# Filling rep straight from dt and u in SBUF, and the second product by x behind the routing of rows

## The reference, cut to what matters

```python
xn   = layernorm(x)
xc   = silu(conv4(xn @ W_in[:1024].T));  gate = silu(xn @ W_in[1024:].T)
ts, Bm, Cm = split(xc @ W_x.T)               # each normalised by its rms
dt   = softplus(ts @ W_dt.T + b_dt)
# for each step: state = state * exp(dt * A) + (dt * xc) * B ;  y = sum over 16 states of state * C
s    = ((y + xc * D) * gate) @ W_out.T
out  = x + s * silu(mixture_of_experts(xn))
```

## Time and profile before

| | us |
|---|---|
| median of 3 runs (1052.16 to 1054.01) | 1053.31 |
| the profiled execution | 1050.33 |
| its span, first to last instruction | 1048.4 |
| DVE busy in the span | 983.2 |
| POOL busy | 904.9 |
| PE busy | 853.0 |
| ACT busy | 728.4 |

### The profile page before, as it was taken

How to read it: one execution, slowest core, us unless ns; L and a number is a source line. 1 busy time by engine, 2 the same in 40 slices (tenths; PEclk the granted TensorE clock), 3 DMA queues, 4 the chain that set the end, 5 groups by cost and what they waited for, 6 DMA issues and landing times.

```text
span 1048.4 us, 10364 instructions
## 1 busy us (share of the span) xinstructions
PE 853.0 (81%) x2756; PEld 317.2 (30%) x2756; DVE 983.2 (94%) x1027; ACT 728.4 (69%) x1281; POOL 904.9 (86%) x320
## 2 busy tenths in 40 slices
PE   8945458989878998999746859989888979988478
PEld 5321113333323343333211313333323323323123
DVE  6779999999999999999999899999999997999996
ACT  3656757888877767888664566888778775767543
POOL 0616899989989998998898988899988989999996
PEclk9986669999989999999976869999999998999778
DMA  9948559887779666675843753866548575664735
GB/s 335 350 154 311 203 200 354 294 298 272 264 271 336 226 226 243 240 276 203 282 116 144 212 209 121 309 236 233 203 178 308 204 255 191 237 237 171 283 54 144
DMA packets 86585, 245.93 MB, mean 235 GB/s; under 512 B 9344, under 2 KB 10752, under 8 KB 79872
## 3 DMA queue, kind: packets, MB, share of 16 engines
q1 hardware_dynamic: 67712, 197.03, 53.0%
q10 hardware_dynamic: 12672, 31.46, 7.6%
q0 software_dynamic: 6144, 16.78, 6.0%
HBM read 183.11 MB, written 62.13 MB: 234 GB/s over the span
## 4 chain that ended last, share of the span: by engine, by line
POOL 22%; DVE 21%; PE 20%; issue 12%; ACT 12%; DMA 10%; SPq 2%; ACTq 0%; DVEq 0%; POOLq 0%
POOL drive L605 13%; DVE sc_ps L1207 7%; DMA rep<-rep_rows 5%; POOL drive L618 4%; ACT sc_ps L818 4%; DVE drive L1207 4%; DVE drive L1217 4%; PE x_ps L1532 3%; PE dt_ps L1460 3%; DMA rep_rows<-dtu 3%; PE f_ps L1485 3%; PE y_ps L1500 2%; PE x_ps L1396 2%; POOL slot_x L569 2%; POOL moe L590 1%
## 5 line engine op out<-in xcount | busy, mean ns | idle before, releaser
L605 POOL TENSOR_TENSOR drive<-rep,b_all 128x2048 f32<-128x2048 f32 x127 | 579.6, 4603 | 37.6 <-DMA rep<-rep_rows 34.0
L818 ACT ACTIVATE sc_ps<-rep,a_neg 128x512 f32<-128x512 f32 x512 | 332.2, 681 | 101.8 <-DVE drive L1217 72.1
L1500 PE MATMUL y_ps<-drive,stack 128*32 128x512 f32 x1024 | 151.6, 668 | 104.1 <-DVE drive L1217 66.2
L618 POOL TENSOR_TENSOR drive<-drive,c_all 128x1024 f32<-128x1024 f32 x92 | 219.8, 2389 | 11.8 <-ACT state L797 9.7
L1207 DVE TENSOR_TENSOR_SCAN sc_ps<-sc_ps,state,drive 128x512 f32<-128x512 f32 x164 | 202.5, 1272 | 5.6 <-ACT sc_ps L818 3.9
L1207 DVE TENSOR_TENSOR_SCAN sc_ps<-sc_ps,drive 128x512 f32<-128x512 f32 x164 | 193.5, 1214 | 10.2 <-ACT sc_ps L818 6.1
L1217 DVE TENSOR_TENSOR drive<-sc_ps,c_all 128x1024 f32<-128x1024 f32 x164 | 199.2, 1215 | 2.8
L1485 PE MATMUL f_ps<-w_ring,xT_slot 128*128 128x512 f32 x368 | 173.0, 614 | 23.4 <-ACT xT_slot L828 22.9
L1460 PE MATMUL dt_ps<-xnT,w_g 128*128 128x512 f32 x232 | 125.1, 689 | 24.1 <-ACT dtu L785 24.1
L1207 DVE TENSOR_TENSOR_SCAN drive<-sc_ps,state,drive 128x512 f32<-128x512 f32 x92 | 113.7, 1267 | 6.6 <-ACT sc_ps L818 6.6
L1207 DVE TENSOR_TENSOR_SCAN drive<-sc_ps,drive 128x512 f32<-128x512 f32 x92 | 109.7, 1208 | 2.0 <-POOL drive L605 0.9
(11 more groups left out here) (189 smaller groups left out, 1048.8 us busy)
## 6 DMA issues: line engine op xcount, KB each, us to landing
rep<-rep_rows SPq DMA_DIRECT2D x128, 512.0 KB, 6.2
w_ring<-wring SPq DMA_DIRECT2D x46, 1024.0 KB, 6.3
rep_rows<-dtu ACTq DMA_DIRECT2D x32, 512.0 KB, 3.1
x_slot<-slot_x SPq DMA_DIRECT2D x46, 256.0 KB, 6.7
slot_rows<-y_slot ACTq DMA_DIRECT2D x46, 256.0 KB, 4.4
w_g<-wg_in SPq DMA_DIRECT2D x32, 256.0 KB, 7.1
w_x<-wx_in SPq DMA_DIRECT2D x24, 256.0 KB, 4.3
slot_x<-zeros SPq DMA_DIRECT2D x1, 5888.0 KB, 20.6
```

The lines of the kernel that those rows point to most:

```text
L605: pool.tensor_tensor(drive[:, m % RING, :, :], rep[:, n % 2, :, 1, :], b_all[:, q:q + 1, :].broadcast_to([P, NR, TC]), ALU.mult).then_inc( ...
L618: pool.tensor_tensor(drive[:, m % RING, 0:2, :], drive[:, m % RING, 0:2, :], c_all[:, q:q + 1, :].broadcast_to([P, 2, TC]), ALU.mult).then ...
L818: act.activation(sc[:, r, :], rep[:, n % 2, r, 0, :], ACT.Exp, scale=a_neg[:, lo:lo + 1]).then_inc(decay_ok, 1)
L1500: last = pe.matmul(y_ps[CH * r:CH * (r + 1), :], stack[:, :], drive[:, m % RING, r, :], start=False, stop=(m % NQ == NQ - 1))
```

## The change

`rep_rows` in DRAM, `keep_rows` and the semaphore `s_dtu` are gone. spread(k) waits for `dt_ok` and `dt_cp`, that is, for u and dt in `dtu`, and its four transfers read 32 partitions each of `dtu` in SBUF, each row four times. `dtu` may now be written again only when all of `rep` for k - 1 has landed, so times_x(k) and keep_dt(k) wait for `rep_landed(k - 1)`. Before the loop, times_x(1) moves from ahead of route_rows to behind it.

```diff
             def spread(k):
-                sp.wait_ge(s_dtu, 16 * (k + 1))
+                sp.wait_ge(dt_ok, k + 1)
+                sp.wait_ge(dt_cp, k + 1)
                 if k >= 2:
                     sp.wait_ge(decay_ok, UNITS * (k - 1))
                     drives_done(sp, NQ * (k - 1))
                 for r in range(NR):
-                    rows = rep_rows[k % 2, CH * r:CH * (r + 1), :].rearrange("c (o f) -> c o f", o=1)
+                    rows = dtu[CH * r:CH * (r + 1), :, :].rearrange("c k (o t) -> c o (k t)", o=1)
                     sp.dma_start(rep[:, k % 2, r, :, :].rearrange("p k t -> p (k t)"),
                                  rows.broadcast_to([CH, NG, 2 * TC])).then_inc(s_rep[k % 2][r // 2], 16)
...
             def keep_dt(k):
                 act.wait_ge(dt_ok, k + 1)
                 if k:
-                    act.wait_ge(s_dtu, 16 * k)
+                    rep_landed(act, k - 1)
                 act.copy(dt, dt_ps[:, :]).then_inc(dt_cp, 1)
...
-            def keep_rows(k):
-                act.wait_ge(dt_cp, k + 1)
-                act.wait_ge(dt_ok, k + 1)
-                if k >= 2:
-                    rep_landed(act, k - 2)
-                act.dma_start(rep_rows[k % 2], dtu[:, :, :].rearrange("p k t -> p (k t)")).then_inc(s_dtu, 16)
...
                 dve.wait_ge(x_ok, k + 1)
                 if k:
-                    dve.wait_ge(s_dtu, 16 * k)
+                    rep_landed(dve, k - 1)
                 dve.tensor_tensor(u, dt_ps[:, :], xy[:, c % 2, t, :], ALU.mult).then_inc(dt_ok, 1)
...
             route_ranks()
-            step_sizes(1)
+            larger_part(1)
+            less_rounding(1)
+            plus_log(1)
             route_rows()
+            times_x(1)
             scan(0, 0)
```

More of the change, by code:

```diff
@@ L117, in scan_moe @@
 def scan_moe(nc, x, wx_in, wg_in, wdt_in, wxp, wring, gate_w, means, a_log, conv_w, conv_b, d_skip,
-             route_consts, bc_dram, rep_rows, xn_rows, xnT_rows, slot_x, slot_rows, s_rows, out):
+             route_consts, bc_dram, xn_rows, xnT_rows, slot_x, slot_rows, s_rows, out):
     with ExitStack() as ctx:
@@ L255, in scan_moe @@
         s_wdt = sem("s_wdt")
-        s_dtu = sem("s_dtu")
         s_wr = [sem(f"s_wr{s}") for s in range(2)]
@@ L916, in _ @@
             keep_dt(0)
-            keep_rows(0)
             softplus(1)
@@ L941, in _ @@
                 diagonal(n)
-                if t < NT - 1:
-                    keep_rows(n + 1)
                 store_slot(b, left_slot)
@@ L1685 @@
     bc = nc.dram_tensor("bc_rows", (NCH, 2 * N, TC), F32, kind="Internal").ap()
-    rep_rows = nc.dram_tensor("rep_rows", (2, P, 2 * TC), F32, kind="Internal").ap()
     xn_rows = nc.dram_tensor("xn_rows", (TOK, H), F32, kind="Internal").ap()
@@ L1692 @@
     out = nc.dram_tensor("out", (TOK, H), F32, kind="ExternalOutput").ap()
-    scan_moe(nc, *aps, bc, rep_rows, xn_rows, xnT_rows, slot_x, slot_rows, s_rows, out)
+    scan_moe(nc, *aps, bc, xn_rows, xnT_rows, slot_x, slot_rows, s_rows, out)
     r = run_bass_kernel_spmd(nc, [arrays], core_ids=[0])
```

## The result

| | before | after |
|---|---|---|
| median, us | 1052.91 (4 runs, 1052.16 to 1054.01) | 1105.20 (4 runs, 1098.25 to 1107.38) |
| ratio, 95% interval | | 1.0484, 1.0435 to 1.0534 |
| the profiled execution | 1050.33 | 1106.86 |
| its span | 1048.4 | 1105.0 |

What follows compares the result with a forecast made beforehand. DVE, busy 983.2 of 1048.4 us, was taken as the bound, with only 36.4 us idle between 60 and 1020 to cut. Gains of 1.95, 2.94 and 1.09 summed to 6.0 us: 1044.3 profiled, 1047.3 median, range 1042 to 1059.

Steps and rivals of the forecast that it cites:

- I take no difference for the sum, as write side, size of rows and engines are unchanged: Spread's four transfers: reading 32 SBUF partitions in place of DRAM takes as long as now, 9 to 10 us; 0 added.
- The rival of the half rate: Spread: transfers move at half the top rate, 3.6 us longer; net +3.4 us, 1056.7; chance 0.28.
- POOL's idle time costs only where DVE later runs into POOL's lateness: POOL's 34.0 us in 13 waits for `rep`: they count only where DVE later waits; DVE never waits for `rep` itself.
- The sign turns at about 2.7: Spread: 1 us longer leaves a gain of 5, 2 us longer 2.5; beyond about 2.7 us the change loses.
- The last rival: Reads much slower, a spread over 10 us longer: POOL late at 13 places, some 1 us each, 1068; chance 0.05.
- Items 1 and 3 to 5 of the sum: DVE idle time that goes: at the start 1.95 us, at 545 us 0, at 834 us 2.94, at 908 us 1.09.
- items 1 and 4: Start: rep(0) and rep(1) sooner, DVE's waits for POOL go, 1.95 us; 834 us: hop leaves the chain, 2.94 us.
- item 5: 908 us: POOL's 1.09 us wait goes, and the chain runs on POOL to DVE's scan at 1004.82; 1.09 us.
- more comes back: Less DRAM traffic and ACT's 0.33 us per tile shorten DVE's waits: some 5 us more, 1042; chance 0.10.
- The added wait: times_x(k) and keep_dt(k) waiting for `rep` of k - 1: hidden by the scans, or by route_rows at k = 1; cost nothing.
- DVE waiting for POOL at 135: Sign that the forecast is wrong; the forecast had DVE's 0.19 us wait for POOL at 135.11 going.
- a POOL wait of 6 us or more near 554: Sign that the forecast is wrong; the forecast had POOL's 3.23 us wait there unchanged.

Runs made afterwards that it cites:

- e1: After, with each transfer reading every fourth partition of 128 in place of 32 neighbours (channels land in another order): 1042.43 us, ratio 0.9912.
- e2: After, with each transfer reading every second partition of 64 in place of 32 neighbours (channels land in another order): 1060.86 us, one run.
- e10: After, with four read forms by tile: 32 neighbours, step 2 in 64, step 4 in 128, all 128 without repeated rows: 1078.16 us, one run.
- e5: After, reading every fourth partition of 128, with weights reordered and the skip product's diagonal permuted to give the reference's result: 1041.56 us, ratio 0.9904.
- e7: e5 with one write of the rows to DRAM put back, waited for and read by nobody: 1045.8 us, one run.
- e9: e5 with times_x(1) back at its old place ahead of route_rows: 1040.83 us, ratio 0.9901.
- e3: Before, with only times_x(1) moved behind route_rows: 1049.25 us, 10 runs, ratio 0.9983.
- e11: After, with times_x(1) back at its old place ahead of route_rows: 1115.47 us, one run.
- e13: After, with ACT's queue issuing the second half of rep(0) beside SP, which issues the first: 1102.14 us, one run.
- e8: e7 with a second write of the rows to DRAM, issued by SP and waited for before the spread: 1076.8 us, one run.
- e12: e8 with a third write of the rows to DRAM, waited for before the spread: 1123.5 us, one run.

## Why the prediction was wrong, step by step

**The step that failed first: "I take no difference for the sum, as write side, size of rows and engines are unchanged".** The source side was what changed. The source ran at 199 GB/s in place of 425, and the one index that spreads each transfer's rows over all partitions brings 379 back (e1, with e2 and e10 beside it). The rival of the half rate had the mechanism right.

**The size of that term.** Its 3.6 us came from 341 GB/s now and half of 430 then. The gap of the halves gives 2.1 MB at 425 and at 199: 4.9 and 10.5 us, 5.6 more; the mean spread grew by 7.1. Where the other 1.5 come from wasn't followed. The 341 was a mean that held gaps, so it was the wrong base to halve.

**The price of a late rep, the larger error.** "POOL's idle time costs only where DVE later runs into POOL's lateness" priced single places: the rival's own numbers rise from -6.0 to +3.4 over 3.6 us, 2.6 for each. At 7.1 us that is +12.5, and +52 was measured. What it missed is that PE's `y_ps` waits for POOL and that the next tile's step sizes stand behind `y_ps`, so that lateness comes back to the spread and is no longer a matter of places. "The sign turns at about 2.7" should have been: at the slack of the loop. Before, at 13.8 us and with 13 waits of POOL, 9 of them under 3 us, stood about at the knee, which the fast reads put between 13.0 and 16.0. PE's clock, which falls while PE waits for POOL and makes the sums behind it slower, isn't in the prediction either. The last rival ("much slower, 1068") had the same fault, and by its own terms, 13 places at 1 us on 1056.7, it would be 1070.

**Items 1 and 3 to 5 of the sum** didn't come about in after: DVE waits 3.82 us for POOL near 141 and 2.94 near 621, POOL waits 2.73 at 905. With the fast read (e5) items 1 and 4 came: POOL starts at 96.95 in place of 101.66, and the waits at 135, 144 and 852 are gone, and of DVE's 4.04 near 878 there is 0.94 left, now for POOL. Of item 5 POOL's 1.09 went, but DVE's wait behind it is there with 2.82 us at 998.56, against 1.69. Altogether e5 gains 10 us where the sum had 6.0, of which the hop itself is 4 to 5 (e7 against e5 and e9) and the move up to 2 (e3; with the fast read it isn't needed). The rest lies between e7 and before, 7.3 us on one chip at nearly the same latency (13.0 and 13.8); part of it may be the reads of DRAM that are gone, which the prediction counted at nothing and the rival "more comes back" at 5. It wasn't taken apart.

**What was right.** The first issue comes within 0.1 us of the end of dt's copy in 18 of 32 tiles; in the others SP was still behind another load or at an issue of one. The added wait stays hidden by the scans, 4.6 us or more over in every tile but the first, where rep(0) at 79.8 is later than 76.9 and costs 2.9 us. The move is harmless, and with the slow read it seems needed (e11, one run). The signs named as wrong, "DVE waiting for POOL at 135" and "a POOL wait of 6 us or more near 554", both stand in the trace: 3.82 us at 141, and 8.49 us at 597.24, which is the tile whose wait was at 554.67 before (another tile waits 6.54 at 522).

**Left open.** Why step 2 in 64 partitions issues in 5.5 to 5.8 us and neighbours in 7.1 to 7.4 when the halves come nearly equally far apart; e13's question; what part of after's time SP's longer issues have, which the line of the fast reads doesn't bound, since SP stands longer in e8 and e12 than in after; and what part PE's clock has.

## What to carry to other kernels

Before a transfer is given another source, ask which partitions each single transfer of it reads, and spread them over all 128 (a stride, with the order of the weights turned to match) in place of a block of neighbours. Then look for the loop: follow the late buffer through its consumers until one of them feeds the next fill of the same buffer, add up one turn, and compare it with the pace of the busiest engine. While the turn is shorter than that pace a microsecond is worth little (about 2 us over 32 tiles here); once it is longer, it is paid in tile after tile (10 to 17 us here). So a kernel that shows small waits in many tiles may already stand at the knee. And look at the granted clock behind the waits of the loop: what stands in it can run slower than before.

## What the runs showed of the hardware that was not expected

- A transfer from SBUF to SBUF that reads each row four times: 199 GB/s from 32 neighbouring partitions (after), 209 from every second of 64 (e2), 379 from every fourth of 128 (e1; by POOL's two starts in e5 2.78 us for 1.05 MB, 377). From DRAM it was 425 (before). These are rates between the two halves of the first spread.
- Reading a row four times costs nothing beside reading four rows: 3.45 against 3.83 us for four issues, and 8.8 against 8.9 us to the last landing (e10).
- With slow transfers under way the issuing queue is held: four issues take 7.74 us in place of 2.46, and the next transfer's issue, another load, 2.48 us in place of 0.62 (before's issue of `c_all` at 70.70).
- The same four issues take 3.5 to 3.8 us in the mean from SBUF at the fast rate (e7, e5) and 2.5 from DRAM, so even the good version holds SP a microsecond longer.
- While PE waited 7.05 us for POOL, its granted clock fell from 1.00 (2.4 GHz) to 0.50 (1.2 GHz), and the ten matmuls behind the wait ran at 0.50 (after, 460 to 464 us).
